# DLRM tower, one core: the first two tiles gathered whole in place of a one-hot search, with the third unit's x spread and turned at later steps

## The reference, cut to what matters

```python
e = jnp.stack([tbl_f[ids[:, f]] for f in range(39)], axis=1)          # (2048, 39, 16)
z0 = jnp.einsum('bid,bjd->bdij', e, e).reshape(B, 16, 39 * 39)
cur0 = relu(jnp.einsum('bdk,kl->bld', z0, W0))                        # 128 maps
next_h, direct0 = jnp.split(cur0, 2, axis=1)                          # 64 and 64
z1 = jnp.einsum('bid,bjd->bdij', e, next_h).reshape(B, 16, 39 * 64)
cur1 = relu(jnp.einsum('bdk,kl->bld', z1, W1))
z = jnp.sum(jnp.concatenate([direct0, cur1], axis=1), axis=-1)
h = relu(jnp.concatenate([z, dense_ctx], axis=1) @ W_top1 + b_top1)
y = relu(h @ W_top2 + b_top2) @ W_top3
```

## Time and profile before

| | |
|---|---|
| median of 3 runs (lowest, highest) | 1476.11 us (1474.81, 1478.93) |
| the profiled execution | span 1510.1 us; no time of its own is given beside the span |
| PE, DVE busy in it | 1434.6 us (95%), 1393.3 us (92%) |
| ACT, POOL busy in it | 825.2 us (55%), 939.0 us (62%) |
| DMA | 293.08 MB, mean 194 GB/s |

### The profile page before, as it was taken

One profiled execution on the slowest core, in us unless ns is written; L12 is line 12 of the kernel. 1 busy time (PEld: TensorE's weight loads), 2 busy tenths in 40 slices (PEclk: granted clock), 3 DMA queues, 4 the chain that ended last, 5 costly groups with the idle time before them and its releaser, 6 DMA issues.

```text
span 1510.1 us, 15015 instructions
## 1 busy us (share of the span) xinstructions
PE 1434.6 (95%) x4458; PEld 794.5 (53%) x4458; DVE 1393.3 (92%) x1253; ACT 825.2 (55%) x897; POOL 939.0 (62%) x604
## 2 busy tenths in 40 slices
PE   3179999999999999999999999999999999999999
PEld 2145555555555555555555555555555555555556
DVE  2179999999999999999999999999999999999993
ACT  0155555655655555655655555655655555655555
POOL 7638888868687786868687786868687780000000
PEclk7589999999999999999999999999999999999999
DMA  5069989999989899999989999899998998898510
GB/s 150 6 160 203 227 216 218 206 220 212 221 198 222 206 217 214 208 223 201 220 203 216 214 212 220 208 213 203 212 216 223 212 210 216 204 222 207 170 35 1
DMA packets 137289, 293.08 MB, mean 194 GB/s; under 512 B 37646, under 2 KB 62878, under 8 KB 137080
## 3 DMA queue, kind: packets, MB, share of 16 engines
q1 hardware_dynamic: 102642, 278.48, 77.2%
q0 software_dynamic: 19200, 4.95, 2.9%
q10 hardware_dynamic: 15366, 8.70, 2.1%
HBM read 284.08 MB, written 7.87 MB: 193 GB/s over the span
## 4 chain that ended last, share of the span: by engine, by line
PE 90%; DVE 4%; issue 2%; another core or an unknown queue 2%; ACT 0%; DMA 0%; DVEq 0%; SPq 0%
PE psB L493 42%; PE psA L493 14%; PE psB L511 7%; PE psB L514 6%; PE psB L518 6%; PE psA L501 2%; PE psA L511 2%; PE psA L514 2%; PE psA L518 2%; PE psB L501 2%; DVE z L902 1%; PE psA L485 1%; DVE z_lo L911 1%; DVE z_split L902 1%
## 5 line engine op out<-in xcount | busy, mean ns | idle before, releaser
L472 POOL DMA_INDIRECT emb<-in_tbl,ids_all x600 | 938.8, 1565 | 309.7 <-issue 178.9
L493 PE MATMUL psB<-z,w 128*128 128x512 f32 x1544 | 690.1, 593 | 5.3 <-DVE z L902 5.3
L767 ACT ACTIVATE z_hi<-z_split 128x1024 fp32r<-128x1024 f32 (+1 forms) x286 | 301.4, 1057 | 464.9 <-DVE z_split L902 372.4
L493 PEld LDWEIGHTS psB<-z,w 128*128 128x128 f32 x1544 | 292.4, 190 | 362.7 <-issue 346.0
L902 DVE TENSOR_TENSOR z<-h_quad,x_lay 128x1024 f32<-128x1024 f32 x354 | 420.5, 1218 | 7.4 <-PE psB L493 5.4
L911 DVE TENSOR_TENSOR z_lo<-z_split,z_hi 128x1024 fp32r<-128x1024 f32 (+1 forms) x286 | 349.3, 1221 | 6.3 <-ACT z_hi L767 3.2
L902 DVE TENSOR_TENSOR z_split<-h_quad,x_lay 128x1024 f32<-128x1024 f32 x222 | 268.4, 1221 | 0.0
L720 ACT ACTIVATE h_quad<-psA 32x1024 f32<-32x1024 f32 x248 | 251.7, 1015 | 6.1 <-DVE feat_side L987 2.4
L493 PE MATMUL psA<-z,w 126*128 126x512 f32 x512 | 241.9, 594 | 0.0
L511 PE MATMUL psB<-z_hi,w_hi 128*128 128x512 f32 x444 | 157.7, 436 | 0.0
L493 PEld LDWEIGHTS psA<-z,w 126*128 126x128 f32 x512 | 97.3, 190 | 98.4 <-issue 92.7
(11 more groups left out here) (113 smaller groups left out, 862.5 us busy)
## 6 DMA issues: line engine op xcount, KB each, us to landing
x_lay<-x_rows SPq DMA_DIRECT2D x1152, 128.0 KB
x_more<-x_rows SPq DMA_DIRECT2D x62, 504.0 KB
bases<-x_rows SPq DMA_DIRECT2D x62, 468.0 KB
x_lay<-x_rows SPq DMA_DIRECT2D x64, 256.0 KB
x_ring<-x_rows SPq DMA_DIRECT2D x31, 504.0 KB
emb<-in_tbl,ids_all POOLq DMA_INDIRECT x600
x_last<-x_rows SPq DMA_DIRECT2D x64, 128.0 KB
x_rows<-x_side ACTq DMA_DIRECT2D x58, 120.0 KB
```

The source lines that it names most:

```text
L472: nc.gpsimd.indirect_dma_start(emb[t % 2][:, f * D:(f + 1) * D], None, tables[f], bass.IndirectOffsetOnAxis(ids_all[:, t, f:f + 1], 0)).th ...
L493: mm = nc.tensor.matmul(ps[:, cs], w[0:k, :], z[WHOLE_NO[place] % NZ][0:k, cs], start=first, stop=last)
L767: nc.scalar.activation(z_hi[n % NS][0:k, 0:cols], z_split[n % NS][0:k, 0:cols], ACT.Copy).then_inc(z_hi_made, 1)
```

## The change

All 39 fields of tiles 0 and 1 are gathered like those of the other tiles. The search, its loads (id rows, table images, constants), buffers, semaphores and waits go. A column of ones, which the last layer took from the search's constants, is loaded by itself. `turn_before(0)` becomes 13, and in unit 0 `spread_x(2)` comes one step before it: it moves from step 7 to step 12, the turn from step 9 to step 13, and `keep_x(2)` from step 11 to step 15.

```diff
 def turn_before(u):
-    return 9 if u == 0 else 2
+    return 13 if u == 0 else 2

-def gathers(t):
-    return F - (HOT_F * HOT_GROUPS[t] if t < HOT_TILES else 0)

 # SP
             sp.dma_start(ids_all[:, 0:1, :], ids[:, 0:1, :].bitcast(U32)).then_inc(ids_loaded, 16)
-            sp.dma_start(hot_row[0], hot_ids[0].bitcast(U32)).then_inc(hot_ids_loaded[0], 16)
-            sp.dma_start(hot_const[:, :], hot_consts).then_inc(hot_const_loaded, 16)
-            sp.dma_start(hot_row[1], hot_ids[1].bitcast(U32)).then_inc(hot_ids_loaded[1], 16)
...
-            sp.wait_ge(hot_tab_loaded[1], 16)
...
+            sp.dma_start(ones[:, :], ones_in).then_inc(ones_loaded, 16)
...
             store_x(0)
             sp.wait_ge(x_stored, 32)
-            sp.wait_ge(hot_found, hot_no(HOT_TILES, 0))
             load_lay(0, 0)

 # GpSimd
-                for f in range(F - gathers(t), F):
+                for f in range(F):
                     nc.gpsimd.indirect_dma_start(emb[t % 2][:, f * D:(f + 1) * D], None, tables[f],

 # TensorE
-            pe.wait_ge(hot_const_loaded, 16)
-            for t in range(HOT_TILES):
-                for q in range(HOT_GROUPS[t]):
-                    spread_hot(t, q)
-                for q in range(HOT_GROUPS[t]):
-                    find_hot(t, q)
             pe.wait_ge(ident_loaded, 16)

 # ScalarE
             def spread_x(u):
                 t = u // 2
-                if t < HOT_TILES:
-                    act.wait_ge(hot_kept, hot_no(t + 1, 0))
-                act.wait_ge(gathered[t % 2], 16 * sum(gathers(n) for n in range(t % 2, t + 1, 2)))
+                act.wait_ge(gathered[t % 2], 16 * F * (t // 2 + 1))
...
-                    if s == turn_before(u) - 2 and u + 2 < UNITS:
+                    if s == turn_before(u) - (2 if u else 1) and u + 2 < UNITS:
                         spread_x(u + 2)
                     if s == turn_before(u) + 2 and u + 2 < UNITS:
                         keep_x(u + 2)
...
-            act.wait_ge(hot_ids_loaded[0], 16)
-            for q in range(len(HOT_BITS)):
-                cols = slice(HOT_COL[q], HOT_COL[q + 1])
-                act.dma_start(hot_tab[:, cols], hot_tables[:, cols]).then_inc(hot_tab_loaded[q], 16)

 # VectorE
-            cut_hot(0)
-            mask_hot(0)
-            for q in range(HOT_GROUPS[0]):
-                make_hot(0, q)
-            cut_hot(1)
-            mask_hot(1)
-            choose_hot(0)
             dve.wait_ge(w0_loaded, 32)
...
-            for q in range(HOT_GROUPS[1]):
-                make_hot(1, q)
-            choose_hot(1)
-            dve.wait_ge(hot_kept, hot_no(HOT_TILES, 0))
+
+            dve.wait_ge(w0_lo_made, 1)
+            dve.wait_ge(w1_lo_made, 1)
```

More of the change, by code:

```diff
@@ L53 @@
 QUAD = P // 4
[L55 to L60, removed]
 FP = mybir.dt.float32
@@ L98, in lay_part @@
     return divmod(s - (s > HALF1) + 1, 2) if s else (0, 0)
-def hot_no(t, q):
-    return sum(HOT_GROUPS[:t]) + q
 def at0(u, s):
@@ L133, in shape_of, with tower @@
     return ROWS if place in RING_AT else P, BANK if half else C
-def tower(nc, ids, tables, hot_ids, hot_tables, hot_consts, ident_in, dense_t, w0_a, w0_b, w1_whole, w1_split, top, top_small, y):
+def tower(nc, ids, tables, ones_in, ident_in, dense_t, w0_a, w0_b, w1_whole, w1_split, top, top_small, y):
     ctx = ExitStack()
@@ L154, in tower @@
         ids_all = sb("ids_all", [P, TILES, F], U32)
[L155 to L158, removed]
+        ones = sb("ones", [P, 1])
         bases = sb("bases", [P, 2 * C])
@@ L204, in tower @@
         more = [x_ring[:, :], x_more[:, 0:C], x_more[:, C:2 * C]]
[L206 to L214, removed]
         base_spread = [r0[:, c * C:c * C + DH * ROWS].rearrange("p (d r) -> p d r", d=DH) for c in range(2)]
@@ L264, in tower @@
         spread = sem("spread")
[L265 to L275, removed]
+        ones_loaded = sem("ones_loaded")
         x_turned = sem("x_turned")
@@ L314, in tower @@
         y_stored = sem("y_stored")
[L316 to L320, removed]
         def stored(u, n):
@@ L638, in _ @@
             pe.wait_ge(small_loaded, 16)
+            pe.wait_ge(ones_loaded, 16)
             def top3_mixed(i):
@@ L645, in top3_mixed @@
                     pe.wait_ge(y_kept, i)
-                nc.tensor.matmul(psB[0:1, K2 * BANK:(K2 + 1) * BANK], hot_ones[:, 0:1], hid2[i % 2][:, 1, :],
+                nc.tensor.matmul(psB[0:1, K2 * BANK:(K2 + 1) * BANK], ones[:, :], hid2[i % 2][:, 1, :],
                                  start=True, stop=True).then_inc(top3_done, 1)
@@ L1003, in body @@
                         sum0(u // 4)
[L1005 to L1034, removed]
@@ L1036, in make_hot @@
-            def make_hot(t, q):
-                dve.wait_ge(hot_spread, hot_no(t, q + 1))
-                cols = slice(q * BANK, (q + 1) * BANK)
-                nc.vector.tensor_scalar(hot[t][:, cols], (psB if t else psA)[:, cols], hot_index, None, ALU.is_equal).then_inc(hot_made, 1)
-            def pick_hot(t, q):
-                dve.wait_ge(hot_found, hot_no(t, q + 1))
-                dve.wait_ge(hot_masked, 2 * t + 2)
-                if hot_no(t, q) >= 2:
-                    dve.wait_ge(hot_kept, hot_no(t, q) - 1)
-                m = 1 << HOT_BITS[q]
-                part = hot_part[q % 2][:, 0:HOT_F * m * D].rearrange("p (f d m) -> p f d m", f=HOT_F, m=m)
-                found = hot_out(t, q).rearrange("p (f d m) -> p f d m", f=HOT_F, m=m)
-                chosen = hot_mask[q // 2][:, t, q % 2 * HOT_F:(q % 2 + 1) * HOT_F, :].unsqueeze(2).to_broadcast([P, HOT_F, D, m])
-                nc.vector.tensor_tensor(part, found, chosen, ALU.mult).then_inc(hot_read, 1)
@@ L1054, in keep_hot @@
-            def keep_hot(t, q):
-                dve.wait_ge(hot_read, hot_no(t, q + 1))
-                m = 1 << HOT_BITS[q]
-                part = hot_part[q % 2][:, 0:HOT_F * m * D].rearrange("p (f d m) -> p f d m", f=HOT_F, m=m)
-                rows = emb[t][:, q * HOT_F * D:(q + 1) * HOT_F * D].rearrange("p (f d) -> p f d", f=HOT_F)
-                nc.vector.tensor_reduce(rows, part, AX.X, ALU.add).then_inc(hot_kept, 1)
-            def choose_hot(t):
-                pick_hot(t, 0)
-                for q in range(1, HOT_GROUPS[t]):
-                    pick_hot(t, q)
-                    keep_hot(t, q - 1)
-                keep_hot(t, HOT_GROUPS[t] - 1)
@@ L1189 @@
     ids = np.asarray(inputs["ids"])[:, order].reshape(TILES, P, F).transpose(1, 0, 2)
-    hot_rows = np.zeros((HOT_TILES, P, HOT_F, P), ids.dtype)
-    for t in range(HOT_TILES):
-        for n in range(HOT_F * HOT_GROUPS[t]):
-            hot_rows[t, QUAD * (n // HOT_F) + n % HOT_F, n % HOT_F] = ids[:, t, n]
-    hot_rows = hot_rows.reshape(HOT_TILES, P, HOT_F * P)
-    hot_tables = np.zeros((P, HOT_COL[-1]), np.float32)
-    for n in range(HOT):
-        q = n // HOT_F
-        m = 1 << HOT_BITS[q]
-        table = np.zeros((P * m, D), np.float32)
-        table[0:len(tables[order[n]])] = tables[order[n]]
-        first = HOT_COL[q] + n % HOT_F * m * D
-        hot_tables[:, first:first + m * D] = table.reshape(P, m, D).transpose(0, 2, 1).reshape(P, m * D)
-    hot_consts = np.zeros((P, P + 17), np.float32)
-    hot_consts[:, 0:P] = 1
-    hot_consts[:, P] = np.arange(P)
-    hot_consts[:, P + 1:] = np.arange(16)
     dense = np.zeros((H, B), np.float32)
@@ L1260 @@
     tower(nc, given("ids", ids), [given(f"tbl_{f}") for f in order],
-          given("hot_rows", hot_rows), given("hot_tables", hot_tables), given("hot_consts", hot_consts), given("ident", np.eye(P, dtype=np.float32)),
+          given("ones", np.ones((P, 1), np.float32)), given("ident", np.eye(P, dtype=np.float32)),
           given("dense", dense), given("w0_a", w0_a), given("w0_b", w0_b), given("w1_whole", w1[:, WHOLE1, :]),
```

## The result

The changed kernel takes 1506.94 us (median of 4 runs, 1506.47 to 1508.86), the kernel before 1475.81 beside it: a ratio of 1.0205, 95% interval 1.0189 to 1.022. That is 31.1 us slower; 24.6 were forecast, and the time lies inside the range. The profiled execution took 1507.08 with a span of 1504.2, so 2.9 us lie around it.

A forecast was written before the change was run, and what follows sets the result against it. TensorE has no gap in the loop, so the start, bound by gathers, and units 0 and 1's waits decide: 1510.1 - 26.8 + 11.3 = 1494.6, plus 6.1 around the span, gives 1500.7 us, 24.6 slower; range 1490 to 1512.

The forecast's parts named there:

- The start: Ahead of unit 0: 39th gather at 50.82, plus 2.0 and 1.10; first copy at 54.0, 20.0 after the timed kernel before.
- Timed runs without the search's stops: Before unit 0's first copy: three stops, 42.5 us together, are absent from timed runs, whose start is 46.8 us earlier.
- The search and its loads cost nothing: At the start: picks, multiplies, table image and id loads lie beside tile 0's 23 gathers, so removing them gains nothing.
- The waits of units 0 and 1: Late gathers, then late loads, make units 0 and 1 wait 11.3 us in place of 6.7 in the kernel before.
- the loads' slack of 4.2: Unit 1's step 3: its load lands at 152.7, 4.2 us ahead of need, so of 15.5 late 11.3 come through.
- Units from 2 on: Loop from unit 2 on: the change does not touch what a unit costs; the period stays 42.5 us.
- A: Start: the search's stops are real in timed runs, so the change removes them, 1476.1 becoming 1460.6; chance 0.07.
- B: Start: about 31 us of stops remain in timed runs, equal to 16 gathers, so no change, 1472 to 1480; chance 0.03.
- C: Around unit 0's start: stops of about 20 or all of 46.8 us return in timed runs, 1521 to 1548; chance 0.06.
- D: Units 0 and 1: the later steps hide everything, only 20.0 of gathers less 6.7 stay, 1489.4 to 1494; chance 0.12.

The follow-up runs named there:

- more search: The kernel before with the search covering all 16 small fields of tile 1 instead of 8, so 8 gathers fewer (592): 1467.73 us, ratio 0.9944.
- tile 0 less 16: The changed kernel with only the 16 added gathers of tile 0 left out, those columns set to zero: 1486.33 us.
- tile 2 less 8: The changed kernel with 8 of tile 2's 39 gathers left out: 1499.52 us (a single run).
- the turn taken earlier: The kernel before, search kept, with unit 0's spread at step 10, turn before step 11 and copy to x_side at step 12: 1475.06 us, ratio 0.9994.

## Why the prediction was right, and where it was off

**The start.** Right. The 39th gather stands at 50.91 (50.82 forecast), the spread and the first copy follow it by 2.4 and 3.6; against 34.07 of the kernel before that is 20.4 later, and 20.0 were in the sum.

**Timed runs without the search's stops.** Right, and it carried the sign: the profiled execution of before held 46.8 us that timed runs don't have. By its span alone the change would have looked 5.9 us faster. The evidence was that a span longer than the timed median can't be a timed run's. The clean span is 1474.4 with 2.4 around it, where 1470.0 and 6.1 were worked out; only their sum was fixed. One reading is wrong and changes nothing: the 0.35 us of work between 30 and 40 that are given to VectorE are those of the weight loads, and VectorE has 0.21.

**The search and its loads cost nothing.** Right: without the 24 gathers the time is that of before.

**The waits of units 0 and 1.** The mechanism was right (a late spread, a late copy behind it, then late loads for unit 1), but both waits were taken too short, and that their difference came out near is luck. From the first copy to unit 1's end (the start of its product with `x_last`) the changed kernel takes 112.9 us, the kernel before 109.8: 3.1 more, where 11.3 - 6.7 = 4.6 were forecast. VectorE's products with `x_last` in units 1 and 2, in the changed kernel, in the kernel before profiled again, and that of unit 1 with more search:

```profile
167.41 0.68 DVE L820 TENSOR_TENSOR z<-h_half,x_last 128x512 f32<-128x512 f32 x1
...
216.60 0.67 DVE L820 TENSOR_TENSOR z<-h_half,x_last 128x512 f32<-128x512 f32 x1
```

```profile
143.84 0.68 DVE L902 TENSOR_TENSOR z<-h_half,x_last 128x512 f32<-128x512 f32 x1
...
186.30 0.68 DVE L902 TENSOR_TENSOR z<-h_half,x_last 128x512 f32<-128x512 f32 x1
```

```profile
135.31 0.68 DVE L902 TENSOR_TENSOR z<-h_half,x_last 128x512 f32<-128x512 f32 x1
```

With more search the third spread waits for no gather and VectorE stops for no load over 1.7 us, and the stretch takes 135.31 - 35.25 = 100.1. Measured from there the wait is 9.7 in the kernel before, 6.7 forecast, and 12.8 in the changed one, 11.3 forecast. Before, tile 1's last gather was issued at 77.56, near the forecast, but landed more than 2.0 us later: the spread began 8.4 after it, and the stop is 9.34. In the changed kernel the stop at step 13 is 5.53, not 8.1, but unit 1's three stops for loads add up to 8.0, where 11.3 - 8.1 = 3.2 were left for them. The term that was off is the loads' slack of 4.2: by the sum step 3's load lands 152.7 - 131.12 = 21.6 us after the third copy to `x_side` begins, in the changed kernel it was 144.88 - 120.19 = 24.7. Step 3 of the kernel before needs it 25.8 after that copy, so a load that takes as long has some 1 us of slack. With tile 1's 8 gathers left out the third spread waits for nothing, and yet unit 1 stops for the three loads, 9.8 us in all, and units 0 and 1 take 110.7: at its later step the copy makes the loads late by itself. That the move is worth something was no part of the sum, and the runs show it worth nothing: 0.7 us in the changed kernel, nothing in that before.

**Units from 2 on.** Wrong, and the step that made the sum short. "The change does not touch what a unit costs from unit 2 on" held from unit 3. Unit 2 takes 49.2 us in the changed kernel and 42.5 before. I had followed the row of gathers to tile 1 and no further, though tile 2's 39 begin where tile 1's end: at 116.09 in place of 79.83. The first gather of tile 2 in the changed kernel, and in the kernel before:

```profile
116.09 0.94 POOL L422 DMA_INDIRECT emb<-in_tbl,ids_all  x1 [0.31 <-issue]
```

```profile
79.83 0.95 POOL L472 DMA_INDIRECT emb<-in_tbl,ids_all  x1 [0.30 <-issue]
```

At the 1.9 us a piece that I had used, and with no time for landing, they would end at 190, and the spread is needed at 184. In fact they went at 1.72 us a piece, and the last took 9.5 to its reader. The spans differ by 29.8: 20.4 at the start, 3.1 in units 0 and 1, 6.7 in unit 2, and 0.4 less in all that follows. The medians differ by 31.1, and 31.1 - 6.7 = 24.4, next to the 24.6 forecast; that this is so close is luck too, since a start 0.4 longer, waits 1.5 shorter and medians 1.3 further apart than the spans make it up. The time lies inside the range because its upper part was there for longer waits in units 0 and 1 and more time around the span; nothing in it was meant for unit 2.

**The rivals.** A and B fall with the second profile of before and the spans of its timed runs. C did not happen: no stop of VectorE without a releaser stands in units 0 to 2 of the changed kernel. D falls too: the later steps hid nothing.

## What to carry to other kernels

When one engine issues a long row of small transfers for several stages ahead, follow the row through every stage until it has slack, and not only to the first wait: a wait removed at one stage comes back at the next as long as the row itself is what bounds. A profiled span above the timed median says that the profile holds something that timed runs don't; subtract it before any term of a sum is made against it. And a piece of work that runs beside such a row is worth what it takes out of the row, here 1.0 us (the 8 of more search) to 1.3 us (the 24) for each gather, so more search was faster and no search slower.

## What the runs showed of the hardware

How long a gather takes until its data are there differed in these traces with how busy the DMA engines were. In the changed kernel the last gather of tile 1 was issued at 114.84 and the spread that waits for it began at 117.17, 2.3 us later. Its last of tile 2 took 9.5:

```profile
181.35 1.42 POOL L422 DMA_INDIRECT emb<-in_tbl,ids_all  x1 [0.30 <-issue]
```

The DMA share of the two stretches of the changed kernel, up to each landing (last two columns: DMA share and GB/s):

```profile
106.00:116.00 10.00, 9.83 (x33) 4.82 (x31) 7.73 (x8) 0.00 (x0) 8.26 (x6) 1.00 0.21 51
...
181.00:190.00 9.00, 8.18 (x20) 3.27 (x18) 4.45 (x4) 3.15 (x4) 7.17 (x7) 1.00 1.04 220
```

The engines were 21% busy in the first and full in the second. In the kernel before, the last gather of tile 1 and the stretch behind it:

```profile
77.56 1.96 POOL L472 DMA_INDIRECT emb<-in_tbl,ids_all  x1 [0.30 <-issue]
```

```profile
78.00:86.00 8.00, 3.63 (x9) 1.32 (x7) 0.71 (x1) 0.03 (x1) 6.25 (x6) 0.87 0.87 202
```

Here it is 8.4 us at 87%. The Trainium skill ("DMA: Bandwidth & Descriptors", the section on the anatomy of a GpSimd-path DMA) gives some 2.0 us beside the data for one; the quiet stretch agrees with its 2.3, the full ones with 8.4 and 9.5 don't. The other runs fall into the same two groups: tile 1's last gather took 2.3 to 2.4 us with the move undone, with tile 0 less 16 and with tile 2 less 8 (DMA share 0.08 to 0.10 until it landed). Tile 2's took 9.2 and 9.4 in the first two of these, and with the turn taken earlier tile 1's took 8.6 and tile 2's 10.0 (0.92 to 1.05). That the loads in front of it make the difference is read from these places; no run took the loads away.
